# Self-attention scores in a decoder layer: from f32 products on masked keys to pairs of f32r products on high keys, low keys and stacked queries

## The reference

```python
q = (x @ Wq.T + bq).reshape(b, n, H, HD)      # H = 16 heads, HD = 16
k = (x @ Wk.T + bk).reshape(b, n, H, HD)
v = (x @ Wv.T + bv).reshape(b, n, H, HD)
score = jnp.einsum('bihd,bjhd->bhij', q, k)
attn = jax.nn.softmax(score / SQRT_D, axis=-1)
o = jnp.einsum('bhij,bjhd->bihd', attn, v).reshape(b, n, f)
return o @ Wo.T + bo
```

## Time and profile before

| | |
|---|---|
| median of 3 runs | 1811.0 us (1810.91 to 1812.59) |
| the profiled execution's own time | 1810.3 us |
| its span, first to last instruction | 1808.5 us |
| granted TensorE clock | 1.00 of full speed (2.4 GHz) in all slices |
| VectorE busy | 1062.4 us (59%), 2213 instructions |
| ScalarE busy | 970.0 us (54%), 1713 instructions |
| GpSimd busy | 429.9 us (24%), 351 instructions |
| DMA | 11 GB/s on average |

### The profile page before, as it was taken

One profiled execution on the slowest core, in us unless ns is written; L12 is line 12 of the kernel. 1 busy time (PEld: TensorE's weight loads), 2 busy tenths in 40 slices (PEclk: granted clock), 3 DMA queues, 4 the chain that ended last, 5 costly groups with the idle time before them and its releaser, 6 DMA issues.

```text
span 1808.5 us, 40567 instructions
## 1 busy us (share of the span) xinstructions
PE 1781.7 (99%) x17278; PEld 1596.0 (88%) x17278; DVE 1062.4 (59%) x2213; ACT 970.0 (54%) x1713; POOL 429.9 (24%) x351
## 2 busy tenths in 40 slices
PE   8999999999999999999999999999999999999998
PEld 7778898988989888898988989898898988989997
DVE  4555565655666556566556656556566656655553
ACT  3345755455555555545455555545545465555553
POOL 2102222222223122222222213222222212212222
PEclk9999999999999999999999999999999999999999
DMA  5000000000000000000000000000000000000000
GB/s 159 10 1 10 2 15 2 10 7 6 11 2 15 2 10 8 1 15 2 10 7 7 10 1 15 2 10 7 1 16 1 10 7 7 10 2 7 1 7 7
DMA packets 20851, 19.65 MB, mean 11 GB/s; under 512 B 9921, under 2 KB 19777, under 8 KB 20289
## 3 DMA queue, kind: packets, MB, share of 16 engines
...
...
## 4 chain that ended last, share of the span: by engine, by line
PE 91%; DVE 4%; POOL 3%; ACT 2%; issue 1%; DMA 0%; POOLq 0%; DVEq 0%; SPq 0%; ACTq 0%
PE ps L458 22%; PE ps L459 20%; PE ps L460 20%; PE ps L546 4%; PE ps L566 3%; POOL h_lo L1396 3%; PE ps L583 2%; PE ps L677 2%; PE ps L693 2%; PE ps L836 2%; PE ps L658 2%; PE ps L768 1%; PE ps L613 1%; PE ps L759 1%; PE ps L500 1%; DVE h_hi L1278 1%
## 5 line engine op out<-in xcount | busy, mean ns | idle before, releaser
L1396 POOL TENSOR_TENSOR h_lo<-h_f,h_hi 128x512 fp32r<-128x512 f32 x256 | 336.2, 1323 | 1125.8 <-DVE h_hi L1278 1125.8
L458 PE MATMUL ps<-w_hi,h_hi 128*128 128x256 f32 x1024 | 299.4, 292 | 6.4 <-POOL h_lo L1396 4.6
L458 PE MATMUL ps<-sl_hi,w_hi 128*128 128x256 f32 x1024 | 302.4, 295 | 1.9 <-DVE sl_lo L1060 1.5
L459 PE MATMUL ps<-w_hi,h_lo 128*128 128x256 f32 x1024 | 289.3, 283 | 0.0
L459 PE MATMUL ps<-sl_hi,w_lo 128*128 128x256 f32 x1024 | 289.2, 282 | 0.0
L460 PE MATMUL ps<-sl_lo,w_hi 128*128 128x256 f32 x1024 | 289.1, 282 | 0.0
L460 PE MATMUL ps<-w_lo,h_hi 128*128 128x256 f32 x1024 | 289.1, 282 | 0.0
L1006 ACT ACTIVATE h_f<-ps 128x512 f32<-128x512 f32 x256 | 149.4, 597 | 143.0 <-PE ps L460 142.4
L1278 DVE CAST h_hi<-h_f 128x512 fp32r<-128x512 f32 x256 | 156.7, 622 | 118.0 <-ACT h_f L1006 117.6
L458 PEld LDWEIGHTS ps<-w_hi,h_hi 128*128 128x128 f32 x1024 | 195.1, 191 | 21.5 <-POOL h_lo L1396 18.5
L458 PEld LDWEIGHTS ps<-sl_hi,w_hi 128*128 128x128 f32 x1024 | 195.0, 190 | 20.2 <-issue 10.5
...
## 6 DMA issues: line engine op xcount, KB each, us to landing
...
```

The costliest lines, as they stand in the source:

```text
L458: te.matmul(o, lhs[0], rhs[0], start=first, stop=False)
L459: te.matmul(o, lhs[1], rhs[0], start=False, stop=False)
L1396: Q_.tensor_tensor(h_lo[:, part, :], h_f[:, part, :], h_hi[:, part, :].bitcast(f32), ALU.subtract)\
```

## The change

Scores are no longer plain f32 products with masked keys. A row tile holds one head: its 32 rows are the 16 rows of queries twice, as high part in rows 0 to 15 and as the low rest in rows 16 to 31 (`qs`). The keys are in both halves of the rows, once as high part (`k_hi`) and once as low part (`k_lo`). Two f32r products, `qs` with `k_hi` and `qs` with `k_lo`, sum up all four partial products.

- PE: per round n, `scores` has 16 f32r products in place of 8 f32 products; `shifted` has 16 f32r in place of 8 f32, with the 8 f32r of the shifts as before.
- ACT: evicts the keys as well (`k_step`, 2 instructions of 128 x 256), and rounds queries and keys to f32r (`qh`, `kh`, one copy of 128 x 1024 each).
- DVE: the four masked-key instructions go. In their place `kd` and `qd` put each head's 16 rows into both halves of its row tile (two stream_shuffle each, 512 elements per partition), `kl` subtracts for the low keys, `qs` makes the stacked queries (128 x 1024 each).
- `k` lies in the space of `xh_a`, `q_hi` in that of `xa_hi`; `qh` therefore waits for the value projection, and the next `xt.1` and `xh.1` wait for the readers.
- The written orders of all engines and of the bank owners are new. In START, 17 idle products stand ahead of `c0.scores.0` where there were 3; all idle products together are 197 where there were 183.

```diff
 ORDER pe, first half of the loop
-        m.lt.0 l.outer.3.0 d.kv m.dispatch.0 l.outer.3.1 c.xt.1 l.comb.3 m.slots.0 d.xt.2 c.k c.q m.hidden.0.0 d.q2
-        c.v m.hidden.0.1 d.scores2.0 m.hidden.0.2 m.hidden.0.3 d.mt2.0 m.lt.1 l.combine.3 d.shifted2.0 m.outer.0.0
-        m.dispatch.1 c.scores.0 d.pv2.0 m.comb.0 m.slots.1 m.outer.0.1 c.mt.0 m.hidden.1.0 c.shifted.0 m.hidden.1.1
+        m.lt.0 l.outer.3.0 d.kv m.dispatch.0 l.outer.3.1 c.xt.1 m.slots.0 l.comb.3 d.xt.2 c.k c.q d.q2 c.v
+        m.hidden.0.0 d.scores2.0 m.hidden.0.1 m.hidden.0.2 d.mt2.0 m.hidden.0.3 m.lt.1 l.combine.3 d.shifted2.0
+        m.outer.0.0 c.scores.0 m.dispatch.1 m.outer.0.1 c.mt.0 m.slots.1 m.comb.0 c.shifted.0 d.pv2.0 m.hidden.1.0
...
 ORDER act
+        m.ed.0 m.ds.0 c.xt.1 m.sl.0 d.xt.2 l.pr.3 l.cb.3 c.k c.q d.q2 c.qh m.ge.0.0 c.kh m.ge.0.1 m.ge.0.2 d.mh2.0
+        m.ge.0.3 m.ed.1 d.ex2.0 m.ds.1 m.ec.0 c.mh.0 m.sl.1 m.cb.0 c.ex.0 m.ec.1 m.ge.1.0 d.xo2.0 m.ge.1.1 m.pr.0
...
 ORDER dve
+        m.cm.0 d.mask d.stats.2 m.edn.0 c.stats.1 d.kv c.xh.1 m.ds.0 d.xh.2 c.xt.1 m.row_max d.xt.2 l.cb.3 m.sl.0
+        c.qd c.v c.kd d.mx2.0 m.hid.0.0 l.pr.3 m.hid.0.1 m.hid.0.2 d.sh2.0 m.cm.1 m.hid.0.3 l.acc.3 c.kl c.qs m.edn.1
+        c.mx.0 m.ds.1 l.finish c.sh.0 m.sl.1 m.cb.0 d.mx2.1 m.hid.1.0 m.hid.1.1 m.pr.0 d.sh2.1 m.hid.1.2 m.cm.2
...
 scores
                 if n == 0:
                     pe.wait_ge(s["q_sb"], nth("q_sb", a, 1))
-                    pe.wait_ge(s["km"], nth("km", a, 1))
+                    pe.wait_ge(s["k_lo"], nth("k_lo", a, 1))
                 for t in range(NT):
-                    for i in range(R):
-                        rows = slice(32 * i, 32 * i + 32)
-                        last = te.matmul(ps[:, 1 + i, t * S:(t + 1) * S], q[rows, c, t * P:(t + 1) * P],
-                                         km[rows, e, c, :], start=True, stop=True)
+                    for keys, first in ((k_hi, True), (k_lo, False)):
+                        for i in range(R):
+                            rows = slice(32 * i, 32 * i + 32)
+                            last = te.matmul(ps[:, 1 + i, t * S:(t + 1) * S], qs[rows, n, t * P:(t + 1) * P],
+                                             keys[rows, n, :], start=first, stop=not first)
 shifted
                 for j in range(NT):
-                    for i in range(R):
-                        rows = slice(32 * i, 32 * i + 32)
-                        te.matmul(ps[:, 1 + i, j * S:(j + 1) * S], km[rows, e, c, j * P:(j + 1) * P], q[rows, c, :],
-                                  start=True, stop=False)
+                    for keys, first in ((k_hi, True), (k_lo, False)):
+                        for i in range(R):
+                            rows = slice(32 * i, 32 * i + 32)
+                            te.matmul(ps[:, 1 + i, j * S:(j + 1) * S], keys[rows, n, j * P:(j + 1) * P], qs[rows, n, :],
+                                      start=first, stop=False)
 ScalarE
+            def k_step(a):
+                act.wait_ge(s["k_ps"], nth("k_ps", a, 1))
...
+                for c in range(C):
+                    last = nc.scalar.activation(k[:, c, :], ps[:, qkv_bank(a, 1), c * S:(c + 1) * S], ACT.Identity,
+                                                bias=bcol[:, 1, c:c + 1])
+                last.then_inc(s["k_ev"], 1)
+            def qh_step(a):
+                act.wait_ge(s["q_d"], nth("q_d", a, 1))
+                act.wait_ge(s["v_ps"], nth("v_ps", a, 1))
+                copy(q_hi[:, :, :], q_d[:, :, :]).then_inc(s["q_h"], 1)
+            def kh_step(a):
+                act.wait_ge(s["k_d"], nth("k_d", a, 1))
+                copy(k_hi[:, :, :], k_d[:, :, :]).then_inc(s["k_h"], 1)
 VectorE
-                for c in range(C):
-                    for e in range(2):
-                        last = V.tensor_scalar(km[:, e, c, :], ps[:, qkv_bank(a, 1), c * S:(c + 1) * S], half[:, e:e + 1],
-                                               bkm[:, e, c:c + 1], ALU.mult, ALU.add)
+            def twice(o, i):
+                for e in range(2):
+                    last = V.stream_shuffle(o[:, e::2, :], i[:, :, :], [HD * e + r % HD for r in range(2 * HD)])
+                return last
+            def qd_step(a):                                  # kd_step: the same on k, k_d
+                dve.wait_ge(s["q_ev"], nth("q_ev", a, 1))
...
+                twice(q_d, q).then_inc(s["q_d"], 1)
+            def qs_step(a):
+                dve.wait_ge(s["q_h"], nth("q_h", a, 1))
+                V.scalar_tensor_tensor(qs[:, :, :], q_hi[:, :, :].bitcast(f32), cols[:, NMASK:NMASK + 1], q_d[:, :, :],
+                                       ALU.mult, ALU.add).then_inc(s["q_sb"], 1)
+            def kl_step(a):
+                dve.wait_ge(s["k_h"], nth("k_h", a, 1))
+                minus(k_lo[:, :, :], k_d[:, :, :], k_hi[:, :, :]).then_inc(s["k_lo"], 1)
```

More of the change, by code:

```diff
@@ new lines @@
+        m.hidden.0.0 d.scores2.0 m.hidden.0.1 m.hidden.0.2 d.mt2.0 m.hidden.0.3 m.lt.1 l.combine.3 d.shifted2.0
+        m.outer.0.0 c.scores.0 m.dispatch.1 m.outer.0.1 c.mt.0 m.slots.1 m.comb.0 c.shifted.0 d.pv2.0 m.hidden.1.0
+        d.scores2.1 m.hidden.1.1 m.hidden.1.2 d.mt2.1 m.hidden.1.3 m.lt.2 m.combine.0 c.pv.0 d.shifted2.1 m.outer.1.0
+        d.tr2.0 m.dispatch.2 c.scores.1 d.pv2.1 m.slots.2 d.ob2.0 m.comb.1 m.outer.1.1 c.mt.1 m.hidden.2.0
+        c.shifted.1 d.tr2.1 m.hidden.2.1 c.scores.2 c.pv.1 m.hidden.2.2 d.ob2.1 m.hidden.2.3 m.lt.3 c.mt.2
@@ L58 @@
+        m.combine.1 d.oproj2 c.shifted.2 m.dispatch.3 c.tr.0 m.outer.2.0 c.ob.0 c.scores.3 c.pv.2 m.slots.3 m.comb.2
+        c.mt.3 m.outer.2.1 c.shifted.3 m.hidden.3.0 d.xt.3 m.combine.2 m.hidden.3.1 m.hidden.3.2 c.pv.3 m.hidden.3.3
+        d.logits.0 c.tr.1 d.logits.1 d.logits.2 c.ob.1 d.logits.3 c.oproj
     """,
     act="""
[L60 to L61 removed]
@@ L87 @@
[L87 to L101, removed]
@@ L102 @@
-        m0.hidden.3.3 c2.tr.1 d1.logits.1 d1.logits.2 c2.ob.1 d1.logits.3 c2.oproj
+        s0.idle.6 c0.mt.2 s0.se_transp.0.0 s0.idle.2 c0.shifted.2 c0.tr.0 s0.idle.3 c0.ob.0 s0.idle.1 c0.scores.3
+        c0.pv.2 s0.se_transp.0.1 s0.idle.4 c0.mt.3 s0.idle.4 c0.shifted.3 s0.idle.8 c0.pv.3 s0.idle.2 c0.tr.1
+        s0.se_transp.1.0 s0.idle.2 c0.ob.1 s0.idle.2 c0.oproj s0.idle.3 d0.kv s0.se_transp.1.1 s0.idle.7 d0.xt.2
+        s0.idle.5 d0.q2 s0.idle.3 c1.xt.1 d0.scores2.0 s0.idle.1 c1.k d0.mt2.0 c1.q d0.shifted2.0 c1.v s1.idle.2
@@ new lines @@
+        d0.scores2.1 d0.pv2.0 s1.idle.3 d0.mt2.1 s1.idle.6 d0.shifted2.1 d0.tr2.0 s1.idle.3 d0.ob2.0 s1.idle.1
+        c1.scores.0 d0.pv2.1 s1.idle.3 d0.tr2.1 s1.idle.4 c1.mt.0 s1.idle.4 d0.ob2.1 c1.shifted.0 d0.oproj2 s1.idle.1
+        c1.scores.1 c1.pv.0 s1.idle.6 c1.mt.1 s1.idle.5 c1.shifted.1 s1.idle.4 d0.xt.3 s1.idle.6 d0.logits.0
+        d0.logits.1 d0.logits.2 d0.logits.3 s1.idle.3 m0.lt.0 c1.scores.2 c1.pv.1 s1.idle.6 c1.mt.2 s1.idle.1
+        m0.dispatch.0 c1.shifted.2 c1.tr.0 m0.slots.0 c1.ob.0 c1.scores.3 c1.pv.2 m0.hidden.0.0 c1.mt.3 m0.hidden.0.1
@@ new lines @@
+        c1.shifted.3 d1.kv m0.hidden.0.2 s1.idle.1 c1.pv.3 s1.idle.2 c1.tr.1 m0.hidden.0.3 c1.ob.1 s1.idle.2 c1.oproj
+        m0.lt.1 m0.outer.0.0 m0.dispatch.1 m0.outer.0.1 c2.xt.1 m0.slots.1 m0.comb.0 c2.k c2.q m0.hidden.1.0
+        m0.hidden.1.1 c2.v d1.xt.2 m0.hidden.1.2 m0.hidden.1.3 m0.combine.0 m0.lt.2 c2.scores.0 d1.q2 m0.outer.1.0
+        c2.mt.0 m0.dispatch.2 c2.shifted.0 m0.slots.2 m0.comb.1 d1.scores2.0 m0.outer.1.1 d1.mt2.0 m0.hidden.2.0
+        d1.shifted2.0 c2.pv.0 m0.hidden.2.1 d1.scores2.1 d1.pv2.0 m0.hidden.2.2 d1.mt2.1 m0.combine.1 d1.shifted2.1
@@ L123 @@
[L123 to L127, removed]
@@ L138 @@
     pe="""
-        m-2.lt.0 l-3.outer.3.0 m-2.dispatch.0 d-1.kv m-2.slots.0 l-3.comb.3 l-3.outer.3.1 m-2.hidden.0.0
-        m-2.hidden.0.1 d-1.xt.2 m-2.hidden.0.2 m-2.hidden.0.3 m-2.lt.1 l-3.combine.3 d-1.q2 m-2.outer.0.0
-        m-2.dispatch.1 d-1.scores2.0 m-2.outer.0.1 d-1.mt2.0 m-2.slots.1 m-2.comb.0 d-1.shifted2.0 m-2.hidden.1.0
-        m-2.hidden.1.1 d-1.scores2.1 d-1.pv2.0 m-2.hidden.1.2 m-2.hidden.1.3 d-1.mt2.1 m-2.combine.0 m-2.lt.2
-        d-1.tr2.0 m-2.outer.1.0 m-2.dispatch.2 d-1.shifted2.1 d-1.ob2.0 m-2.comb.1 m-2.slots.2 m-2.outer.1.1
@@ new lines @@
+        m-2.hidden.0.1 d-1.q2 m-2.hidden.0.2 m-2.hidden.0.3 m-2.lt.1 l-3.combine.3 d-1.scores2.0 m-2.outer.0.0
+        m-2.dispatch.1 m-2.outer.0.1 d-1.mt2.0 m-2.slots.1 m-2.comb.0 d-1.shifted2.0 m-2.hidden.1.0 m-2.hidden.1.1
+        m-2.combine.0 m-2.hidden.1.2 m-2.hidden.1.3 m-2.lt.2 d-1.pv2.0 d-1.scores2.1 m-2.outer.1.0 m-2.dispatch.2
+        m-2.outer.1.1 d-1.mt2.1 m-2.slots.2 m-2.comb.1 d-1.shifted2.1 d-1.tr2.0 m-2.hidden.2.0 d-1.ob2.0
+        m-2.hidden.2.1 d-1.pv2.1 m-2.hidden.2.2 d-1.tr2.1 m-2.hidden.2.3 m-2.lt.3 d-1.ob2.1 m-2.combine.1 d-1.oproj2
```

204 lines of the change are left out of this document (108 added, 96 removed).

## The result

| | before | after |
|---|---|---|
| median (range) | 1810.95 us (1810.84 to 1812.59) | 1778.66 us (1777.79 to 1779.99) |
| the profiled execution | 1810.3 | 1779.5 |
| granted TensorE clock, mean | 1.00 | 0.996 |

The ratio is 0.9821, 95% interval 0.9806 to 0.9835: 32.3 us faster. The forecast was 1767 with a range of 1758 to 1785; the time is inside the range, but the gain is a quarter smaller than the 43.7 us forecast, and between the two profiled executions it is 30.8.

What follows compares the result with a forecast made beforehand. The loop is bound by what TensorE issues. Loop 41.1 less 2.6 and START 9.5 less 3.3 less 1 make 43.7 us off 1810.3: forecast 1767, range 1758 to 1785 for 8 in 10.

Steps and rivals of the forecast that it cites:

- TensorE gives back 3.16 us per sequence: Score products: f32r rounds at 0.12 us save 0.40 per scores and 0.39 per shifted, 50.6 us for 16 sequences.
- Rival 2: Score products: TensorE is bound by issuing tiled products, 59 ns each; slower by 23.7 us, about 1838; chance 0.06.
- VectorE and ScalarE: Engine loads: VectorE gets 51 us more in all, ScalarE 47; both stay near 65% of an iteration, neither becomes the bound.
- rival 3: The shuffles on VectorE cost 2.8 us each, cross-attention's maximum comes 6 us late; about 1845 us; chance 0.03.
- The longer way is tight at scores.0: Loop, projections to scores: qs is ready at 13.0 us, scores.0 due at 13.4; kl waits for GpSimd; fits narrowly.
- the 0.4 us: Loop, scores.0: the time to spare between the end of qs at 13.0 and scores.0 due at 13.4.
- The 0.2 us per iteration for what is late: Loop: allowance for steps late in some iterations, 13 x 0.2 = 2.6 us.
- the prediction's last sign of being wrong: Loop: the means of the cast and of GpSimd rise and outer waits; no size given.
- rival 1: Loop order fits badly, late by the lock or a softmax step; 1 us per iteration, 10.4 more, 1777; chance 0.23.
- START: 9.5 less 3.3 less 1: START: 9.5 us gained on three sequences' attention, less 3.3 for 14 more idle products, less 1 for waits elsewhere.
- Elsewhere in START ... I add 1 us: START, away from the first scores: 1 us of loss, where TensorE already waits 1.3 of 20 us.
- FINISH 0: FINISH: no self-attention and another order, so no gain, give or take 2 us.

Runs made afterwards that it cites:

- e1: The changed kernel with both steps of the splitting of w2 put back ahead of START's first cross-attention norm, as before the change; 1773.86 us, ratio 0.9794.
- e2: e1 with seven idle TensorE products added in three gaps of START near 197 to 201 us; 1771.91 us, on another chip 1773.38 us.

## Why the prediction was right, and where it was not

- *TensorE gives back 3.16 us per sequence.* Right. Scores in the timeline after, four rounds of four records:
```profile
831.67 0.39 PE L553 MATMUL ps<-k_hi,qs 32*128 32x256 f32 x4
831.89 0.28 PE L553 MATMUL ps<-k_lo,qs 32*128 32x256 f32 x4
832.01 0.28 PE L553 MATMUL ps<-k_hi,qs 32*128 32x256 f32 x4
832.13 0.29 PE L553 MATMUL ps<-k_lo,qs 32*128 32x256 f32 x4
832.34 1.07 PE L590 MATMUL ps<-pt,vz 128*32 128x256 f32 x16
```
  0.22 to the second round, then 0.12 each, and 0.09 more before the next step: 0.67 for 0.68 forecast; `shifted` has a median of 0.916 for 0.92. Rival 2 is ruled out: four f32r products start every 0.12 us, 30 ns each; what was 59 ns in the earlier trace rows was two records. PE busy is 1739.7 for 1737.
- *VectorE and ScalarE.* The new operations cost what was set. Groups of VectorE by shape, after:
```profile
L1329 DVE CAST h_hi<-h_f 128x512 fp32r<-128x512 f32 x256 | 175.4, 691 | 67.0 <-ACT h_f L1034 66.2
L1315 DVE TENSOR_SCALAR edt<-edt,crec 128x256 f32<-128x256 f32 x128 | 47.9, 416 | 2.3
L1088 DVE TENSOR_TENSOR k_lo<-k_d,k_hi 128x1024 fp32r<-128x1024 f32 x16 | 28.6, 1786 | 0.0
L1148 DVE STREAM_SHUFFLE q_d<-q 128x512 f32<-128x512 f32 x32 | 22.5, 752 | 0.0
L1148 DVE STREAM_SHUFFLE k_d<-k 128x512 f32<-128x512 f32 x32 | 22.1, 739 | 0.0
L1161 DVE SCALAR_TENSOR_TENSOR qs<-q_hi,consts,q_d 128x1024 fp32r<-128x1024 f32 x16 | 21.4, 1339 | 0.0
```
  A shuffle is 0.75 us (0.65 taken; rival 3 is ruled out). But VectorE got 99 us more, not 51. The missing 48, small differences left out, are 9 of `k_lo` at 1.79 in place of 1.22, 19 of the casts to `h_hi`, 8 of `edt`, 13 of two of the `xh` groups of L1136. All but `k_lo` are unchanged work. The casts before:
```profile
L1278 DVE CAST h_hi<-h_f 128x512 fp32r<-128x512 f32 x256 | 156.7, 622 | 118.0 <-ACT h_f L1006 117.6
```
  It is time spent waiting for GpSimd, which the rows count as busy. In the trace after, 124 of the 256 casts start while a GpSimd instruction runs; each of them ends 0.28 to 0.31 us behind it, and they take 0.42 to 1.43 us, where the other 132 take 0.41 to 0.43. Of the 16 `k_lo`, 14 start so and take 1.83 us or more, the other two 1.22. The prediction reckoned with this lock for `kl` and `qs` alone, and put it down to two inputs from SBUF, though its own maximum of 1427 ns was a cast's, which has one. The Trainium skill (SBUF — State Buffer, "Who interferes with whom") lists cast and tensor_scalar, too, among what can contend in their two-port modes, and says the one issued first blocks the other wholly; the 5.89 us above agree. ScalarE: 48 us more for 47 forecast.
- *The longer way is tight at scores.0.* TensorE never waits for `qs` in the loop, so the 0.4 us were enough; `kl` waits for GpSimd in 14 of 16 sequences, as foreseen. The 0.2 us per iteration for what is late were too few: waits rose from 0.14 to 0.59. Half of the prediction's last sign of being wrong came true: the casts' mean rose from 622 to 691 ns and `outer` waits 0.18 us per iteration for the low part (793.20 above), while GpSimd's mean stayed at 1323. One of the three waits is the lock. Timeline after, VectorE and GpSimd:
```profile
840.55 1.26 DVE L1315 TENSOR_SCALAR edt<-edt,crec 128x256 f32<-128x256 f32 x2
```
```profile
840.13 1.27 POOL L1446 TENSOR_TENSOR h_lo<-h_f,h_hi 128x512 fp32r<-128x512 f32 x1 [0.69 <-DVE h_hi L1329]
```
  The two `edt` end 0.4 us behind GpSimd's end at 841.40, and dispatch.3 waits 0.24 for them. It is rival 1, at a third of its price (the loop is 3.5 us off its forecast, the rival said 10.4). The account closes: TensorE's busy time per iteration fell by 3.13 us, its waits grew by 0.45, and the iteration is 2.68 shorter.
- *START: 9.5 less 3.3 less 1.* The step that failed. "Elsewhere in START ... I add 1 us" was set without going through what the new order moves past what. It moved a 4.57 us GpSimd instruction to stand beside a VectorE step on the critical way; e1 shows 4.7 to 7.4 us for it, by the trace that it is held against, and e2 another 1.7 for the half clock near 200. Of the 10.7, 1.6 stay unexplained at the least. The step held no term for the clock, which fell to half twice in START.
- *FINISH 0.* It gained 1.3, within the 2 allowed; its cause was not looked for. That the total fell inside the range is owed to the range's upper part, which was meant for rival 1, a late loop: what used up most of it was START.
